# Exact attention scores in two row halves of TensorE, with the order of the work around them changed

## The reference

```
x1 = x + tanh(g_xattn) * (attention(layernorm(x), ctx; 16 heads of 8, 120 keys) @ Wo + bo)
h  = rms(layernorm(x1)) * n1
q, k = per-head rms of h @ wq.T, h @ wk.T;  v = h @ wv.T
x2 = layernorm(x1) + causal_attention(q, k, v; 16 heads) @ wo.T       (first 32 channels get nothing)
xf = rms(x2) * n2;  gates = top 2 of softmax(xf @ gate.T), renormalised
moe = sum over 4 experts of gate_e * expert_e(xf)                      (first 32 channels get nothing)
out = x1 + tanh(g_ffn) * (x2 + moe)
```

## Time and profile before

| | |
|---|---|
| median of 3 runs | 1074.19 us (1071.29 to 1077.75) |
| profiled execution | 1072.52 us, of it 1070.7 us from the first to the last instruction (the span) |
| busy, share of the span | TensorE 94%, VectorE 74%, ScalarE 69%, GpSimd 32%, weight loads 58% |
| granted TensorE clock, mean | 0.987 of full speed |

### The profile page before, as it was taken

The page is one execution under the profiler, slowest core; times in us unless marked ns, Lnnn a source line. Parts: engine busy times, 40 slices in busy tenths (PEclk is TensorE's granted clock), DMA queues, the critical chain, the costliest instruction groups (busy, mean ns, idle before and its releaser), DMA issues.

```text
span 1070.7 us, 26205 instructions
## 1 busy us (share of the span) xinstructions
PE 1004.9 (94%) x8649; PEld 626.3 (58%) x8649; DVE 789.2 (74%) x2172; ACT 736.1 (69%) x1334; POOL 337.8 (32%) x463
## 2 busy tenths in 40 slices
PE   6678799999999999999999999999999999999898
PEld 5445456566665656666565666656566665655565
DVE  8667777877787787778778777877877777774723
ACT  6466677676777767677776767777676777767453
POOL 5615134051513405151240515124051512404130
PEclk9989899999999999999999999999999999999999
DMA  7433432233343233434323343432234343221200
GB/s 233 134 106 130 136 112 93 90 102 127 115 142 111 90 92 103 127 115 140 109 92 92 106 127 115 136 109 93 90 111 127 115 135 109 82 67 62 69 1 20
DMA packets 77317, 114.28 MB, mean 107 GB/s; under 512 B 7776, under 2 KB 40160, under 8 KB 77152
## 3 DMA queue, kind: packets, MB, share of 16 engines
q1 hardware_dynamic: 76800, 111.53, 33.0%
q10 hardware_dynamic: 480, 2.26, 0.6%
HBM read 58.97 MB, written 53.74 MB: 105 GB/s over the span
## 4 chain that ended last, share of the span: by engine, by line
PE 64%; DVE 15%; ACT 11%; issue 7%; DMA 1%; SPq 1%; POOL 0%; DVEq 0%; ACTq 0%
PE ps_pv L1362 9%; PE ps_w L1388 9%; PE ps_s2a L1341 7%; PE ps_s2b L1341 5%; PE ps_s2a L1400 5%; PE ps_s2b L1407 4%; PE ps_t L1224 4%; ACT probs L951 4%; PE ps_w L1407 3%; DVE mpadB L1091 3%; PE ps_w L1273 3%; DVE mpadA L1091 3%; PE ps_t L1375 2%; PE ps_w L1224 2%; PE ps_w L1305 2%
## 5 line engine op out<-in xcount | busy, mean ns | idle before, releaser
L951 ACT ACTIVATE probs<-ps_s2a 120x512 f32<-120x512 f32 (+1 forms) x256 | 153.4, 599 | 73.1 <-PE ps_s2a L1341 64.7
L1091 DVE TENSOR_REDUCE mpadB<-ps_w 128x4 f32<-128x512 f32 x240 | 148.8, 684 | 24.9 <-PE ps_w L1305 24.9
L1091 DVE TENSOR_REDUCE mpadA<-ps_w 128x4 f32<-128x480 f32 x224 | 131.5, 651 | 38.0 <-PE ps_w L1305 38.0
L951 ACT ACTIVATE probs<-ps_s2b 120x512 f32<-120x512 f32 (+1 forms) x256 | 153.6, 600 | 0.0
L818 POOL TENSOR_SCALAR_AFFINE_SELECT probs<-probs 128x1024 f32<-128x1024 f32 x128 | 139.8, 1092 | 0.0
L1388 PE MATMUL ps_w<-W,hid 128*128 128x96 f32 x976 | 122.5, 279 | 1.0 <-DVE split_k L985 0.9
L1388 PEld LDWEIGHTS ps_w<-W,hid 128*128 128x128 f32 x976 | 114.9, 193 | 10.4 <-issue 4.9
L786 POOL TENSOR_TENSOR rB<-vrB,neg_half 128x4 f32<-128x4 f32 x16 | 16.1, 1007 | 207.2 <-DVE veB L978 207.2
L1341 PE MATMUL ps_s2a<-qdA,kstA 128*120 128x512 f32 x128 | 68.7, 537 | 7.0 <-ACT probs L951 3.1
L1400 PE MATMUL ps_s2a<-hid,W 128*128 128x512 f32 x152 | 74.4, 604 | 0.0
L1120 DVE SCALAR_TENSOR_TENSOR ym<-ps_w,gates,ym 128x96 f32<-128x96 f32 x184 | 45.7, 311 | 38.5 <-PE ps_w L1388 38.5
(11 more groups left out here) (279 smaller groups left out, 2166.7 us busy)
## 6 DMA issues: line engine op xcount, KB each, us to landing
scratch_Aq<-split_q SPq DMA_DIRECT2D x48, 256.0 KB, 2.4
qdA<-scratch_Aq SPq DMA_DIRECT2D x64, 192.0 KB
scratch_Bq<-split_q SPq DMA_DIRECT2D x48, 256.0 KB, 2.4
scratch_Bk<-split_k SPq DMA_DIRECT2D x48, 256.0 KB, 2.9
qdB<-scratch_Bq SPq DMA_DIRECT2D x64, 192.0 KB
kstB<-scratch_Bk SPq DMA_DIRECT2D x64, 192.0 KB
scratch_Ak<-split_k SPq DMA_DIRECT2D x48, 240.0 KB, 2.3
kstA<-scratch_Ak SPq DMA_DIRECT2D x64, 180.0 KB
```

Of the source, the lines that this page charges most:

```text
L951: nc.scalar.activation(probs[0:k, slot_of(part, *index), :], bank[0:k, :], ACT.Exp, scale=SCALE if part == "A" else 1.0).then_inc(done, 1)
L1091: nc.vector.tensor_reduce(pair[:, :, c, b % 2] if halves else mneg[p][:, :, c, b], bank[:, 0:HT * k].rearrange("p (h k) -> p h k", h=HT), ...
```

## The change

Exact scores: the rows of `qd` and `kst` are laid out anew. Heads 0 and 1 of each c take rows 0 to 47 with the maximum (and the ones) in row 48; heads 2 and 3 take rows 64 to 111 with row 112. `qd` has 2 x 128 columns for each (b, c) where it had 4 x 128. A pair of (b, c), (b, c + 1) is done by four matmuls of 256 columns, two in each half of the rows; the first half's two heads of both c go to bank `s2a`, the other's to `s2b`. A pair starts when both banks are drained, and `values` wait for both banks of a pair. The exps and masks keep their shapes.

The order: `values` of a b are split in `early_values` (c = 0, 1) and `late_values` (c = 2, 3) in most places; downs 0 and 3 are split in `head` (two sequences) and `rest`; quads, `qk`, B `sums`, D `squares`, D `out` and `xfT` move. B `init` waits for D `out` (`y_ready`). The clears of `qd` at the start become smaller. The core of the diff:

```diff
+HEADED = (0, 3)
 def self_attention():
-    return (one("N", "load", 0, None) + one("N", "ctx", 0, None) + exact("D", 0, 0) + one("B", "hT") + down(1) + exact("D", 0, 2)
-            + one("B", "qk", 0) + one("B", "qk", 1) + one("B", "qk", 2) + one("B", "qk", 3)
-            + exact("D", 1, 0) + estimate("A", 0) + exact("D", 1, 2)
-            + one("B", "squares", 0, None) + values("D", 0)
-            + exact("D", 2, 0) + estimate("A", 1) + exact("D", 2, 2)
-            + values("D", 1) + one("B", "sums", 0, None) + down(0)
-            + exact("D", 3, 0) + one("D", "oT", 0, "t") + estimate("A", 2) + exact("D", 3, 2)
-            + one("A", "base", 0, None) + values("D", 2) + one("D", "nT", 0, "t") + one("B", "root", 0, None))
+    return (one("N", "load", 0, None) + one("N", "ctx", 0, None) + exact("D", 0, 0) + one("B", "hT") + down(1)
+            + exact("D", 0, 2) + one("B", "qk", 0) + one("B", "qk", 1) + early_values("D", 0)
+            + exact("D", 1, 0) + one("B", "qk", 2) + one("B", "qk", 3) + late_values("D", 0)
+            + exact("D", 1, 2) + one("B", "squares", 0, None) + estimate("A", 0) + early_values("D", 1)
+            + exact("D", 2, 0) + head(0) + late_values("D", 1)
+            + exact("D", 2, 2) + one("B", "sums", 0, None) + rest(0) + one("D", "oT", 0, "t")
+            + exact("D", 3, 0) + early_values("D", 2) + estimate("A", 1) + one("D", "nT", 0, "t") + late_values("D", 2)
+            + exact("D", 3, 2) + one("A", "base", 0, None) + one("B", "root", 0, None))
 def second_experts():
-    return (fill("M", "e2_l2", 0) + one("D", "wo", 0, "t") + one("B", "scale", 0, None) + fill("M", "e2_l2", 1)
-            + estimate("A", 3) + values("D", 3) + fill("M", "e3_up", 0) + one("D", "oT", 1, "t") + fill("M", "e3_up", 1)
-            + one("N", "stats", 0, None)
-            + one("D", "nT", 1, "t") + one("A", "mT") + fill("M", "e2_l3", 0) + one("N", "norm", 0, None) + one("D", "wo", 1, "t")
-            + one("D", "out", 0, None) + one("B", "qT") + one("B", "kT") + one("D", "squares", 0, None)
-            + fill("M", "e2_l3", 1, "w"))
+    return (one("D", "wo", 0, "t") + early_values("D", 3) + estimate("A", 2) + fill("M", "e2_l2", 0) + one("B", "scale", 0, None)
+            + late_values("D", 3) + fill("M", "e2_l2", 1) + estimate("A", 3) + fill("M", "e3_up", 0) + one("D", "oT", 1, "t")
+            + fill("M", "e3_up", 1) + one("N", "stats", 0, None) + one("A", "mT") + fill("M", "e2_l3", 0) + one("D", "nT", 1, "t")
+            + one("B", "qT") + one("B", "kT") + one("N", "norm", 0, None) + one("D", "wo", 1, "t") + fill("M", "e2_l3", 1, "w"))
 def cross_attention():
-    return (exact("A", 0, 0) + one("B", "v") + down(2) + exact("A", 0, 2) + one("N", "xT")
-            + exact("A", 1, 0) + estimate("B", 0) + exact("A", 1, 2)
-            + one("D", "norm", 0, None) + one("B", "init", 0, None) + one("B", "copy", 0, None) + values("A", 0)
-            + exact("A", 2, 0) + estimate("B", 1) + exact("A", 2, 2)
-            + values("A", 1) + down(3) + one("M", "store", 0, None) + one("D", "xfT")
-            + exact("A", 3, 0) + one("A", "oT", 0, "t") + estimate("B", 2) + exact("A", 3, 2)
-            + values("A", 2) + one("D", "logits") + one("A", "nT", 0, "t"))
+    return (exact("A", 0, 0) + one("B", "v") + down(2) + exact("A", 0, 2) + one("N", "xT") + one("D", "squares", 0, None)
+            + estimate("B", 0) + one("D", "out", 0, None)
+            + exact("A", 1, 0) + values("A", 0) + one("D", "norm", 0, None) + one("B", "init", 0, None) + one("B", "copy", 0, None)
+            + exact("A", 1, 2) + head(3) + early_values("A", 1)
+            + exact("A", 2, 0) + rest(3) + one("M", "store", 0, None) + late_values("A", 1)
+            + exact("A", 2, 2) + one("D", "xfT") + estimate("B", 1)
+            + exact("A", 3, 0) + one("A", "oT", 0, "t") + early_values("A", 2) + estimate("B", 2)
+            + exact("A", 3, 2) + one("D", "logits") + late_values("A", 2) + one("A", "nT", 0, "t"))
...
-        qd = {p: sb("qd" + p, [P, HT, NT, TOK], F32R) for p in "AB"}
+        qd = {p: sb("qd" + p, [P, HT // 2, NT, TOK], F32R) for p in "AB"}
...
-        M_ROW = HD * SPLIT * HT
+        HALF_ROWS, M_ROW = P // 2, HD * SPLIT * HT // 2
...
+        def rows_of_head(j):
+            first = j // 2 * HALF_ROWS + j % 2
+            return slice(first, first + M_ROW, 2)
...
-                        to_tile = qd[to][at, j, :, :] if o == "q" else kst[to][at, :, :]
+                        to_tile = qd[to][at, j % 2, :, :] if o == "q" else kst[to][at, :, :]
...
                             dve.wait_ge(xf_ready, g)
+                            dve.wait_ge(y_ready, g)
...
-                        for bk, v in st.drains([], key):
-                            pe.wait_ge(drained[bk], v)
-                        o = bank[0:k, :].rearrange("p (h q) -> p h q", h=HT)
-                        mm(o, kst[p][:, c, b * k:(b + 1) * k], qd[p][:, :, c, b * P:(b + 1) * P],
-                           start=True, stop=True).then_inc(done, 1)
+                        if c % 2:
+                            continue
+                        tiles = [(part, "s2", (b, c + half)) for half in range(2)]
+                        for tile in tiles:
+                            for bk, v in st.drains([], tile):
+                                pe.wait_ge(drained[bk], v)
+                        for cc in range(2):
+                            for half in range(2):
+                                rows = slice(half * HALF_ROWS, half * HALF_ROWS + M_ROW + 1)
+                                o = psum[st.bank[tiles[half]]][0:k, cc * 2 * P:(cc + 1) * 2 * P].rearrange("p (h q) -> p h q", h=2)
+                                ins = mm(o, kst[p][rows, c + cc, b * k:(b + 1) * k], qd[p][rows, :, c + cc, b * P:(b + 1) * P],
+                                         start=True, stop=True)
+                                if cc:
+                                    ins.then_inc(filled[st.bank[tiles[half]]], 1)
...
-                        sources = [(part, "s2", index)] if part == "A" else []
+                        sources = [(part, "s2", (b, c // 2 * 2 + half)) for half in range(2)] if part == "A" else []
```

More of the change, by code:

```diff
@@ L89, in estimate, with values, early_values, late_values @@
     return [(part, "s1", (b, c), rings[c]) for c in range(NT)]
-def values(part, b):
-    return [(part, "pv", (b, c), "pv" if b % 2 and c == NT - 1 else None) for c in range(NT)]
+def values(part, b, first=0, last=NT):
+    return [(part, "pv", (b, c), "pv" if b % 2 and c == NT - 1 else None) for c in range(first, last)]
+def early_values(part, b):
+    return values(part, b, 0, PACK)
+def late_values(part, b):
+    return values(part, b, PACK, NT)
 def one(part, work, index=0, ring="w"):
@@ L206, in fourth_group @@
     return (one("D", "mL", 0, "t") + of_parts("NABD", self_attention())
-            + one("D", "wo", 0, "t") + estimate("A", 3) + values("D", 3) + one("D", "oT", 1, "t") + one("A", "mT")
-            + one("B", "scale", 0, None) + one("D", "nT", 1, "t") + one("D", "wo", 1, "t") + one("D", "out", 0, None)
+            + one("D", "wo", 0, "t") + early_values("D", 3) + one("B", "scale", 0, None) + estimate("A", 2) + late_values("D", 3)
+            + one("D", "oT", 1, "t") + estimate("A", 3) + one("A", "mT") + one("D", "nT", 1, "t") + one("D", "wo", 1, "t") + one("D", "out", 0, None)
             + exact("A", 0, 0) + one("B", "qT") + one("B", "kT") + exact("A", 0, 2) + one("N", "stats", 0, None) + one("B", "v")
-            + one("D", "squares", 0, None) + one("N", "norm", 0, None) + one("N", "xT")
+            + one("D", "squares", 0, None) + one("N", "norm", 0, None) + one("N", "xT") + estimate("B", 0)
             + cross[cross.index(("A", "s2", (1, 0), "s2")):] + experts)
@@ L236, in last_self_keys @@
             + one("D", "squares", 2, None) + estimate("B", 1) + fill("M", "e2_l3", 1)
-            + fill("M", "down", 2, "pv") + estimate("B", 2) + one("D", "norm", 2, None) + one("B", "init", 0, None) + one("B", "copy", 0, None)
-            + one("D", "xfT", 0, "t") + fill("M", "down", 3, "pv") + one("M", "store", 0, None) + one("B", "v", 0, "f") + one("D", "logits", 0, "t")
+            + down(2, "pv") + estimate("B", 2) + one("D", "norm", 2, None) + one("B", "init", 0, None) + one("B", "copy", 0, None)
+            + one("D", "xfT", 0, "t") + down(3, "pv") + one("M", "store", 0, None) + one("B", "v", 0, "f") + one("D", "logits", 0, "t")
             + fill("D", "e1_w1", 0) + fill("D", "e1_w2", 0) + one("D", "keep", 0, None) + estimate("B", 3)
@@ L1377, in step @@
                         ins.then_inc(done, 1)
-                    elif work == "fill" and index[0] == "down":
-                        h = DOWN_OF[index[1]]
-                        if index[1] in (0, 1):
-                            sources = st.settled(*(("f",) if st.parts == "M" and index[1] == 1 else ("w", "f")))
-                        else:
```

(22 more changed lines are left out.)

29 lines of the change are left out of this document (15 added, 14 removed).

## The result

The changed kernel takes 1166.39 us (median of 4 runs, 1165.46 to 1169.96) against 1073.89 us: a ratio of 1.0862, 95% interval 1.0837 to 1.0887. Slower was forecast, but 1108 us with a range of 1050 to 1135: the loss was put at 35 us and is 92. The profiled execution took 1169.96 us, its span is 97.5 us longer than that of before.

A forecast was written before the change was run, and what follows sets the result against it. TensorE's stream was taken to bound the kernel. Shapes +0.8, cross waits +2.2, self part -0.3 a pass, taken as +2.5, gave +30 over 12 passes; ramp and tail added 2.5 and 3: 1108 us, range 1050 to 1135.

The forecast's parts named there:

- the term for ramp and tail: Ramp and tail: +2.5 us for last ramp and first tail step, +3 for pairs directly behind pairs.
- the quads' waits: Cross attention: three moved estimate quads wait for copies or reductions, 1.1, 1.2 and 1.0 us a pass.
- A pair streams in half the time: Exact scores: row halves run side by side, 0.22 us a pair for 0.46, saving 3.84 us a pass.
- Changes of shape, +0.20 for entering the halves: TensorE: each entry into row halves empties the pipeline, +0.20 us; all shape changes cost +4.6 a pass.
- the rival without emptying: Exact pairs: entering and leaving row halves costs nothing, -6.0 us a pass, about 1033 us; chance 0.12.
- the one with serial weights: Exact pairs: the halves' weights load one after the other, +56 us, about 1160 us; chance 0.08.
- The net of +0.8 a pass: Bare TensorE time of a pass: shape changes +4.6 us against 3.84 saved by streaming.
- Exact pairs 0.2: Cross attention: a pair needs both banks drained, so it waits 0.2 us for ScalarE in each of two places.
- The self part: Self-attention and second experts: most old ScalarE waits go, new ones come, 2.1 us against 2.4, -0.3 a pass.
- the entry: Start of self-attention and experts: waits around D(0,0), `hT` and down1 stay at 0.8 us, as before.
- The sum of a pass: Loop pass: 0.8 + 2.2 - 0.3 = +2.7 us, taken as +2.5, over 12 passes +30.
- Half each: Last ramp step and first tail step: each loses half of a pass's loss, together +2.5 us.

The follow-up runs named there:

- e2: The kernel before with its old order of work, but exact scores in two row halves: 1118.99 us, ratio 1.0401.
- e6: The changed kernel with small identity matmuls inside the three masked quads' waits of the cross part, full passes only: 1153.99 us, ratio 1.0739.
- e1: The changed kernel's new order of work, with the old exact scores over full rows: 1134.42 us, ratio 1.0550.
- e9: The changed kernel with the cross part reordered and the old order in the ramp's fourth step, halves kept: 1108.17 us, ratio 1.0327.
- e4: The changed kernel with small identity matmuls in TensorE's waits of the ramp: 1163.82 us, ratio 1.0819.
- e7: The changed kernel with the two halves of each exact pair issued one after the other: 1165.61 us, ratio 1.0830.

## Why the prediction was wrong, step by step

Of the 97.5 us, 59.4 lie in the 12 passes, where 30 were forecast, and 38.1 in ramp and tail, where 5.5 were. Two steps failed: TensorE's clock, for which the sum has no term, and the term for ramp and tail. The direction came out by mechanisms that the forecast named, the quads' waits above all.

- **A pair streams in half the time**: right. The halves run side by side, their steps 0.12 apart.
- **Changes of shape, +0.20 for entering the halves**: right in kind and size (0.18 behind a quad); neither the rival without emptying nor the one with serial weights came. The net of +0.8 a pass cannot be read off as work, since a matmul slowed by a wait counts as busy: e2's pass has 2.8 us less work, the changed kernel's 0.8 less. As whole passes the halves cost +1.0 in the old order and +0.4 in the new one.
- **The quads' waits**: right. B0 1.17 (forecast 1.1), B1 1.34 (1.2), B2 1.07 (1.0). Exact pairs 0.2, as forecast, once or twice a pass.
- **The self part**: right in its new waits. Early D1 0.20, quad A1 0.42 behind down0's update (the forecast's own numbers give 0.3), `nT` 0.25. Of the entry, forecast at 0.8, the idle time shows 0.23, ahead of `hT`. Missed: the logits wait 0.33 behind B2, whose banks are still being reduced.
- **The sum of a pass**: +2.5 was forecast; a pass without half clock is +3.4 (65.93), the average +4.5. The term put at nothing is the clock: "its mean granted clock is 1.00" was read from the pass before and carried over to one with three waits of over 1 us within 13 us. The passes with and without a stretch size that at 1.2 us, and e6 shows that the waits make most of them. Of the 29 us missed in the passes some 11 are the 0.9 of each pass, 13 the stretches and 6 the first pass, in which 13.7 us stand at half clock.
- **Ramp and tail, +5.5**: the largest miss. The ramp lost 30.7 us to the first pass and the tail 7.4. I took the ramp for a place where TensorE waits on others, so that only some pairs cost. Two things were not seen. In the second step, at half clock, TensorE's own work set much of the time: it was busy 26.8 us and not 17.7, with about as much idle time, and `values` took 1.91 us (1.07 before). And the fourth step has no expert layers: the third quad, moved behind half a `values`, holds up the fourth quad, the maxima, their load and the first cross pair. "Half each" of a pass's loss was taken for it; it lost 14.0, which the order made (e1 against e2) and e9 gets back.

What stays open: why the clock fell at 18.3 us and not in the kernel before, with as much work ahead; as e6 shows, steps with the same instructions come out at one clock or another, so some of the ramp's loss in the profiled execution is chance. What makes up the third step's 4.9 us was not separated; e4 gives the clock about 1 of them, and the pairs' wait for two exps is argued, not shown. The tail's 7.4 were not taken apart either. They seem to go with the halves: the tail takes 171.3 us in e1 and 184.0 in e2 against 170.2, but e2's has a clock of 0.92.

## What to carry over

An order that puts a long wait where there was none is priced twice: by the wait, and by TensorE's clock in the work behind it; so look at how full the stretch ahead is, not only at how long the pass gets. Cost each moved step in every stage that runs the list, above all in a ramp step in which the work that covers it is missing. And a matmul split into halves that need two banks at once ends the alternation of the banks, one filled while the other is drained: count the time between such pairs, not only their streaming.

## What was not expected of the hardware

- The clock fell behind waits of 0.5 to 1.35 us each with work between them (6.54 of 9.30 us busy ahead of one fall), not only behind long idle times; 11 small matmuls in three such waits held it up in 8 of 11 passes.
- Two early stretches with 1.47 of 4.10 and 1.48 of 3.98 us of work led to full clock in one kernel and to half clock in the other; two kernels with the same first instructions differ by 7 us at the end of the third step (102.7 against 95.4 us).
- Matmuls in different row halves start side by side even when they are issued one half after the other (425.37 and 425.38 in e7). The Trainium skill ("TensorE: Matmul & The Clock Gate", Part 3, The mechanism) has matmuls start strictly in their order; by these rows they don't here.
